# Windowed attention and top-1 experts on one core: the output product as a three-term split with its low part from VectorE, global rows turned ahead of the second pair's queries, and the values of a pair one window at a time

## What is computed

```python
q, k, v = (x @ w.T + b for w, b in ...)          # (2, 2048, 16 heads, 16)
scores = zeros(S, S) per head
scores[window n, window n] = q k^T * scale       # 16 windows of 128 per sequence
scores[gi, gi] += q[gi] k[gi]^T * scale          # gi = 0, 32, 64, ...
out = softmax(scores) @ v @ wo.T + bo
x = layernorm(x + out)
top1 = argmax(x @ Wg.T)
h = gelu((norm(x) * ln_scale[e] + ln_bias[e]) @ W1[e] + b1[e])   # e = top1
x = layernorm(x + h @ W2[e] + b2[e])
```

## Time and profile before

| | us |
|---|---|
| time, median of 3 runs (lowest, highest) | 457.8 (457.61, 458.39) |
| the profiled execution | 456.82 |
| its span, from first to last instruction | 455.1 |
| TensorE busy with matmuls | 413.0 |
| VectorE busy | 331.6 |
| ScalarE busy | 220.6 |
| GpSimd busy | 220.8 |

### The profile page before, as it was taken

How to read it: one execution, slowest core, us unless ns; L and a number is a source line. 1 busy time by engine, 2 the same in 40 slices (tenths; PEclk the granted TensorE clock), 3 DMA queues, 4 the chain that set the end, 5 groups by cost and what they waited for, 6 DMA issues and landing times.

```text
span 455.1 us, 14887 instructions
## 1 busy us (share of the span) xinstructions
PE 413.0 (91%) x5894; PEld 350.1 (77%) x5907; DVE 331.6 (73%) x806; ACT 220.6 (48%) x423; POOL 220.8 (49%) x300
## 2 busy tenths in 40 slices
PE   5968898999999999999999999998799998998981
PEld 4838787898898898898898888776587777877871
DVE  7792578666666666666768888654578899799876
ACT  3413355445446446446446546566664555544320
POOL 5331244535545545545545666436743477458531
PEclk9998999999999999999999999999999999999996
DMA  8650734000000000000002000000000011011112
GB/s 242 193 174 7 211 128 131 26 2 23 23 0 23 23 0 23 23 0 23 23 0 73 24 4 2 3 3 1 0 4 1 0 48 46 5 41 48 46 48 93
DMA packets 21705, 20.35 MB, mean 45 GB/s; under 512 B 3117, under 2 KB 21666, under 8 KB 21666
## 3 DMA queue, kind: packets, MB, share of 16 engines
q1 hardware_dynamic: 17428, 15.60, 10.9%
q10 hardware_dynamic: 4238, 4.22, 3.0%
HBM read 15.41 MB, written 4.41 MB: 44 GB/s over the span
## 4 chain that ended last, share of the span: by engine, by line
PE 69%; DVE 20%; issue 6%; POOL 2%; ACT 1%; DVEq 0%; POOLq 0%; ACTq 0%
PE ps L1413 10%; PE ps L1367 10%; PE ps L1680 7%; PE ps L1376 7%; PE ps L1390 6%; PE ps L1511 6%; PE ps L1358 5%; PE ps L1336 5%; PE ps L1396 4%; PE ps L1381 2%; PE ps L1612 2%; POOL attn_t L594 2%; DVE num_t L1159 2%; DVE row_max_t L1136 1%; DVE hm_part L1287 1%
## 5 line engine op out<-in xcount | busy, mean ns | idle before, releaser
L835 ACT ACTIVATE probs<-ps 128x1024 f32<-128x1024 f32 x64 | 62.1, 1023 | 74.1 <-PE ps L1381 74.1
L1136 DVE TENSOR_REDUCE row_max_t<-ps 128x16 f32<-128x2048 f32 x31 | 70.9, 2288 | 12.7 <-PE ps L1367 12.7
L1680 PE MATMUL ps<-w_part,hm_part 128*128 128x256 f32 x384 | 54.9, 292 | 4.2 <-DVE hm_part L1287 3.7
L1367 PE MATMUL ps<-k_part,q_part 32*128 32x128 f32 x1584 | 51.6, 274 | 3.3 <-issue 1.3
L1367 PEld LDWEIGHTS ps<-k_part,q_part 32*128 32x128 f32 x1584 | 46.9, 186 | 9.5 <-issue 7.0
L594 POOL TENSOR_TENSOR attn_t<-num_t,rden_t 128x256 f32<-128x256 f32 x32 | 19.9, 623 | 70.2 <-DVE rden_t L1162 70.2
L1680 PEld LDWEIGHTS ps<-w_part,hm_part 128*128 128x128 f32 x384 | 48.4, 191 | 7.2 <-DVE hm_part L1287 4.5
L1511 PE MATMUL ps<-xh_parts,w_part 128*128 128x512 f32 x192 | 52.6, 409 | 0.0
L685 ACT ACTIVATE pvT_t<-ps 128x512 f32<-128x512 f32 x34 | 20.4, 599 | 56.5 <-PE ps L1390 53.6
L554 POOL TENSOR_TENSOR q_part<-qf,q_part 128x512 fp32r<-128x512 f32 x32 | 41.5, 1300 | 11.6 <-ACT q_part L685 11.6
L582 POOL TENSOR_TENSOR bounds_t<-guard_t,bounds_t 128x16 f32<-128x16 f32 x32 | 7.1, 222 | 76.6 <-DVE guard_t L1148 76.6
(11 more groups left out here) (226 smaller groups left out, 925.9 us busy)
## 6 DMA issues: line engine op xcount, KB each, us to landing
table<-rest_sums SPq DMA_DIRECT2D x4, 1088.0 KB, 6.8
xs<-in_L_attn_x_dram SPq DMA_DIRECT2D x16, 256.0 KB, 2.7
rows<-in_L_attn_x_dram ACTq DMA_DIRECT2D x4, 1024.0 KB, 7.9
out_dram<-yout SPq DMA_DIRECT2D x7, 512.0 KB, 2.8
w<-in_L_ffn_W_dram SPq DMA_DIRECT2D x2, 256.0 KB, 7.5
w<-in_L_ffn_W_dram SPq DMA_DIRECT2D x1, 512.0 KB, 4.7
out_dram<-yout SPq DMA_DIRECT2D x2, 256.0 KB, 2.1
w_raw<-in_L_attn_wq_dram SPq DMA_DIRECT2D x1, 256.0 KB, 2.9
```

The costliest lines, as they stand in the source:

```text
L835: act.activation(probs[:, 2 * h:2 * h + 2, :], ps[:, 2 * h:2 * h + 2, :], ACT.Exp).then_inc(probs_ready, 1)
L1136: dve.tensor_reduce(row_max[:], ps_all, op=ALU.max, axis=AX.X).then_inc(max_ready, 1)
L1367: last = mm(ps[:, u, (2 * c + a) * P:(2 * c + a + 1) * P], q_part[x][quad(u), s, c, a, :], k_part[y][quad(u), s, c, :], start=(i == 0), st ...
L1680: mm(y, hm_part[a][:, 1 - p, f, c * P:(c + 1) * P], w2_part[b][:, f, :], start=(f == 0 and i == 0), stop=False)
```

## The change

- The output product becomes a split product: `wo` gets a high and a low part like the other weights (`weight_high(WO)` on ScalarE, `w_low(WO)` on GpSimd), and `aT` becomes `aT_part`. ScalarE's copy writes the high part, and a new subtraction on VectorE, between guards and queries, writes the low part; `aT_ready` now comes from VectorE.
- On TensorE the 16 transposes of the global rows and `rest_of_windows` stand ahead of the queries of the second pair in step 0. On VectorE the four `lift` instructions and one on `v_rest` move from before step 0 to behind its guards.
- In odd steps `values_of` does one window of the pair at its old place, `second_values` does the other where x was turned, and x is turned ahead of the turned scores.
- In the expert part `hidden_low` of the last chunk of the last group moves from step 8 to the end of step 7, ahead of `finish(3)`, and in step 8 all twelve Newton steps stand ahead of `finish(0)`; they were spread over the four.
- Some tensors change their place: `vec_rows` and `b1_rows` to an early area, and `wT` of wo into `ffn_rows`.

```diff
         x_part = [sb(f"x_part{i}", [P, KC, 2, P], fp32r) for i in range(2)]
-        w_part = [[sb(f"{n}_part{i}", [P, KC, HID], fp32r) for i in range(2)] for n in ("wq", "wk", "wv")]
+        w_part = [[sb(f"{n}_part{i}", [P, KC, HID], fp32r) for i in range(2)] for n in ("wq", "wk", "wv", "wo")]
         rows = sb("rows", [P, NW * HID])
-        woT = sb("woT", [P, KC, HID])
         out_bias = sb("out_bias", [P, HID])
...
         ffn_rows = sb("ffn_rows", [P, 2, FC * GT])
-        wT = [ffn_rows[:, 0, i * KC * HID:(i + 1) * KC * HID].rearrange("p (c n) -> p c n", c=KC) for i in range(3)] + [woT[:]]
+        wT = [ffn_rows[:, 0, i * KC * HID:(i + 1) * KC * HID].rearrange("p (c n) -> p c n", c=KC) for i in range(4)]
 
...
         rden = sb("rden_t", [P, 2, HEADS])
-        aT = sb("aT_t", [P, KC, P])
+        aT_part = [sb(f"aT_part{i}", [P, KC, P], fp32r) for i in range(2)]
         bn6 = sb("bn6", [P, TG, 6])
...
             pool.iota(rank_i[:], pattern=[[-1, EXPERTS]], base=EXPERTS, channel_multiplier=0).then_inc(late_const, 1)
+            w_low(WO)
             attention_steps(pool, step, first=0, split=2 * SLOTS, between=lambda: pool.wait_ge(other_sums_in_table, 16 * (ROUNDS - 1)))
...
             def weight_high(i):
-                act.wait_ge(wqk_ready, i + 1) if i < WV else act.wait_ge(wvo_ready, 1)
+                act.wait_ge(wqk_ready, i + 1) if i < WV else act.wait_ge(wvo_ready, i - WV + 1)
                 copy(w_part[i][0][:], wT[i]).then_inc(w_high_ready, 1)
...
             values_of(0, 0)
+            weight_high(WO)
             act.wait_ge(g_bound, 1)
...
                     act.wait_ge(aT_in_psum, t - 2)
-                    copy(aT[:].rearrange("p c n -> p (c n)"), ps_rao[:, 0:HID]).then_inc(aT_ready, 1)
+                    copy(aT_part[0][:].rearrange("p c n -> p (c n)"), ps_rao[:, 0:HID]).then_inc(aT_high_ready, 1)
                 if not steady and t == 0:
...
             dve.tensor_tensor(out_bias[:], ps_pv[:, 0:HID], out_bias[:], ALU.add).then_inc(out_bias_ready, 1)
-            for j in range(HPU):
-                dve.scalar_tensor_tensor(lift[:, j, :], global_keys[:], lift_row[:, HPU + 1:HPU + 2],
-                                         lift_row[:, j:j + 1].broadcast_to([P, P]), ALU.mult, ALU.subtract)
-            dve.tensor_scalar(v_rest[:].rearrange("r (h e) -> r h e", e=VA)[:, :, DH], pvals[0:2 * NW, 5:6].broadcast_to([2 * NW, HEADS]),
-                              -float(GLOBALS - GPW), float(S - WINDOW), ALU.mult, ALU.add)
 
...
                     dve.tensor_tensor(guard[:, p, :], row_max[:], at_least, ALU.max).then_inc(guard_ready, 1)
+                if not steady and t == 0:
+                    for j in range(HPU):
+                        dve.scalar_tensor_tensor(lift[:, j, :], global_keys[:], lift_row[:, HPU + 1:HPU + 2],
+                                                 lift_row[:, j:j + 1].broadcast_to([P, P]), ALU.mult, ALU.subtract)
+                    dve.tensor_scalar(v_rest[:].rearrange("r (h e) -> r h e", e=VA)[:, :, DH], pvals[0:2 * NW, 5:6].broadcast_to([2 * NW, HEADS]),
+                                      -float(GLOBALS - GPW), float(S - WINDOW), ALU.mult, ALU.add)
                 if older:
...
                 early(1)
+                if old:
+                    dve.wait_ge(aT_high_ready, t - 2)
+                    dve.tensor_tensor(aT_part[1][:].rearrange("p c n -> p (c n)"), ps_rao[:, 0:HID],
+                                      aT_part[0][:].rearrange("p c n -> p (c n)").bitcast(fp32), ALU.subtract).then_inc(aT_ready, 1)
                 if ahead and p == 0:
...
                                              ps[:, 4 + j % 2, 0:HID], ALU.mult, ALU.add).then_inc(ysum_ready, 1)
-                    newtons(3 * j, 3 * j + 2)
+                    if steady or n != NG:
+                        newtons(3 * j, 3 * j + 2)
                     dve.wait_ge(ysum_ready, w + 1)
...
                 for c in range(FC):
-                    if prev and c == 0:
+                    if prev and c == 0 and (steady or n < NG):
                         hidden_low(n - 1, 1 - p, FC - 1)
...
                         hidden_low(n, p, FC - 2)
+                    if not steady and n == NG - 1 and c == FC - 1:
+                        hidden_low(n, p, FC - 1)
+                    if not steady and n == NG and c == 0:
+                        newtons(0, NEWTON_STEPS + 1)
                     if later and c < 2:
...
                         dve.wait_ge(ybn_ready, 4 * n)
-                    newtons(3 * c + 2, 3 * c + 3)
+                    if steady or n != NG:
+                        newtons(3 * c + 2, 3 * c + 3)
                     if not steady and n == 1:
...
                     pe.wait_ge(w_low_ready, 3)
-                for k in range(2):
-                    last = split_product(ps_kv[:, k * HID:(k + 1) * HID], [part[:, :, k, :] for part in x_part], w_part[WV])
-                last.then_inc(v_in_psum, 1)
+                split_product(ps_kv[:, 0:HID], [part[:, :, 0, :] for part in x_part], w_part[WV])
+
+            def second_values():
+                split_product(ps_kv[:, HID:2 * HID], [part[:, :, 1, :] for part in x_part], w_part[WV]).then_inc(v_in_psum, 1)
 
...
                 pe.wait_ge(aT_ready, w + 1)
-                product(ps_rao[:, HID:2 * HID], lambda c: aT[:, c, :], lambda c: woT[:, c, :]).then_inc(o_in_psum, 1)
+                if isinstance(w, int) and w == 0:
+                    pe.wait_ge(w_low_ready, 4)
+                split_product(ps_rao[:, HID:2 * HID], aT_part, w_part[WO]).then_inc(o_in_psum, 1)
 
...
                     sum_windows()
+                if not steady and t == 0:
+                    pe.wait_ge(gs_shifted, B)
+                    pe.wait_ge(max_ready, 1)
+                    for u in range(UNITS):
+                        for i in range(HPU):
+                            last = nc.tensor.transpose(ps[:, u, i * P:(i + 1) * P], dg[:, u, i * P:(i + 1) * P], ident[:])
+                    last.then_inc(gT_in_psum, 1)
+                    rest_of_windows()
                 if not steady and t == 1:
...
                     values_of(t + 1)
+                if live(t + 3, steady) and p:
+                    turn_x(t + 3)
                 if not steady and t == NW - 2:
...
                     last.then_inc(b1_sums_in_psum, 1)
-                if not steady and t == 0:
-                    pe.wait_ge(gs_shifted, B)
-                    pe.wait_ge(max_ready, 1)
-                    for u in range(UNITS):
-                        for i in range(HPU):
-                            last = nc.tensor.transpose(ps[:, u, i * P:(i + 1) * P], dg[:, u, i * P:(i + 1) * P], ident[:])
-                    last.then_inc(gT_in_psum, 1)
-                    rest_of_windows()
                 if not steady and t == 1:
...
                     keys_of(t + AHEAD)
-                if live(t + 3, steady) and p:
-                    turn_x(t + 3)
+                if live(t + 1, steady) and p:
+                    second_values()
                 if pp:
...
             values_of(0)
+            second_values()
             pe.wait_ge(gs_scaled, B)
...
             pe.wait_ge(consts_ready, 1)
-            product(ps_pv[:, 0:HID], lambda c: bv_wide[:, c, :], lambda c: woT[:, c, :]).then_inc(bias_in_psum, 1)
+            product(ps_pv[:, 0:HID], lambda c: bv_wide[:, c, :], lambda c: wT[WO][:, c, :]).then_inc(bias_in_psum, 1)
             attention_steps(pe, step, first=0)
```

More of the change, by code:

```diff
@@ L117, in windowed_attention_then_top1_experts @@
             colvals = early_sb("colvals", [P, 2, 2 * NW])
+            vec_rows = early_sb("vec_rows", [NVEC, HID])
+            b1_rows = early_sb("b1_rows", [FC, P])
         w1_part = [sb(f"w1_part{i}", [P, KC, EXPERTS * EH], fp32r) for i in range(2)]
@@ L192, in windowed_attention_then_top1_experts @@
         nx = sb("newton_x", [P, NW])
-        vec_rows = sb("vec_rows", [NVEC, HID])
         vecT = sb("vecT", [P, KC, NVEC])
         bq_col, bk_col, bv_col = (vecT[:, :, 3 * EXPERTS + i] for i in range(3))
-        b1_rows = sb("b1_rows", [FC, P])
         w1 = sb("w1", [P, KC, EXPERTS, EH])
@@ L361, in windowed_attention_then_top1_experts @@
         aT_in_psum = sem("aT_in_psum")
+        aT_high_ready = sem("aT_high_ready")
         aT_ready = sem("aT_ready")
```

## The result

The changed kernel takes 459.8 us (median of 7 runs, 458.6 to 460.7) against 458.3 us for the kernel before, run beside it (median of 7, 457.5 to 459.0). The ratio is 1.0037, with a 95% interval from 1.0021 to 1.0053: 0.4% slower. The forecast was 450.0 us, with a range from 445.0 to 455.7, so both its size and its sign are wrong.

What follows compares the result with a forecast made beforehand. TensorE was taken to pace the attention loop, with long single waits at start and end. Start -5.5, loop -5.6 and end +3.3 made -7.8 us: 449.0 for the profiled execution, 450.0 for the median, range 445.0 to 455.7.

Steps and rivals of the forecast that it cites:

- Start, -5.5: Up to the scores of window 2: global rows turned earlier, at full clock, gain 5.5 us, bounds 3.4 and 6.5.
- into idle time of both: Start: the split of wo, a ScalarE copy and a GpSimd subtraction, falls into idle time of both engines.
- Loop, even steps, 0: Attention loop: VectorE's added instruction changes nothing in even steps; bad end 0.15 us each, 2 us in all.
- third rival: Even steps: VectorE paces the loop, its added 0.42 us delaying every step, +11.8 us, 467 us in all; chance 0.06.
- Loop, odd steps, -0.4 each: Attention loop: moved values and x shorten 14 odd steps from 8.20 to 7.81 us, 5.6 us in all.
- The old stall is gone: Odd steps: 1.73 us of TensorE work behind the sums covers the 1.75 us until the attention transposes can start.
- End, +3.3: Expert end: Newton chain ahead of window 28's sum idles TensorE 5.3 us; loss 3.3 us, bounds -3 and 4.5.
- Nothing I can price changes: Between loop and end: no change priced; output products there stand behind waits for routing and residuals.
- first rival: Loop gives nothing: row maxima in odd steps and numerators in even ones take back 0.4 us; 455.6 us, chance 0.16.

Runs made afterwards that it cites:

- e4: Changed kernel with the output product in fp32 again (no split, no parts of wo), all else kept: 454.6 us.
- e11: Kernel before with only the global rows turned ahead of the second pair's queries and the lift instructions behind the first guards: 451.9 us.
- e7: Changed kernel with VectorE's new low part, in even steps, ahead of the row maxima instead of ahead of the queries: 458.6 us.
- e8: Changed kernel with the two attention transposes of an odd step behind the scores of the next even step: 455.8 us.
- e1: Changed kernel with both edits of the end undone (last hidden chunk's low part and Newton steps at their old places): 456.7 us.
- e3: Changed kernel with the twelve Newton steps of group 6 behind the sum of window 29, not ahead of that of window 28: 455.1 us.
- e2: Changed kernel with only the Newton steps back in their old places, the last hidden chunk's low part still early: 456.9 us.
- e6: Changed kernel with both windows' values together at the old place and x turned where it was before: 459.2 us.
- e5: Changed kernel with only GpSimd's subtraction for wo moved behind its low part of the first pair's queries in step 0: 457.5 us.
- e9: Changed kernel without the output product's split and with the Newton steps of group 6 behind the sum of window 29: 449.8 us.
- e10: Changed kernel without the split, group 6 Newton steps behind window 29's sum, odd steps' attention transposes behind the next scores: 446.7 us.
- e12: Kernel before with only the output product split (low part on VectorE, parts of wo at the start): 462.2 us.

## Why the prediction was wrong, step by step

- **Start, -5.5: right where the split isn't.** e4 and e11 show its terms (31.34, full clock, window 2 at 46.8 and 47.1). The step that failed is the half-sentence that put the split of wo "into idle time of both" engines. It priced the instruction where it stands, not what it does to its neighbour: 1.32 us on `g_row`, and in this profile 1.63 of clock behind it. From `g_row` on, the change gains 2.42 us, and e4 5.41. The earlier trace rows held the pattern (a 0.17 us instruction at 1.82 beside GpSimd), and the forecast used it at the end but not at the start.
- **Loop, even steps, 0: wrong by 3.2 us.** The step that failed is the wait of the bounds' turning on the numerators: I put it at 0 to 0.15 us and let 0.06 us saved cancel it. Measured, the ordinary even step is +0.15, and in every other one, where VectorE's bounds come 0.17 us later than in the rest (4.33 us after the scores, not 4.16), +0.26 to +0.38: before, a small slack had hidden that difference, and the numerators started 6.18 to 6.20 us after the scores in both. It is the third rival's place at a quarter of its price, but not its wait: the keys did cover the attention transposes of even steps, as I had said against it. e7 shows it by taking the instruction out of the chain, e8 by bringing TensorE there later.
- **Loop, odd steps, -0.4 each: 0.1.** "The old stall is gone" was nearly true (by e8, 0.05 us of it is left in the loop), but I counted it as time gained. The timelines give, from start of the sums to the transposes, 2.43 us before and 2.42 after: the drain, numerators, reciprocal and division take that long whatever TensorE does meanwhile, so the moved values fill that time and don't shorten it. My step had 0.60 + 0.81 + 0.11 + 0.81 = 2.33 there, 0.22 for the transposes (0.34), and 3.95 ahead of the turned scores (4.03). Three terms were small by 0.08 to 0.12, and together they are the missing 0.3; for the transposes itself has 0.41. The whole gain is in front, where 4.13 became 4.03 at the row maxima. That new wait I had forecast at 0.20 us; it is 0.27 (4.03, less 3.76 of scores, weighing, values and x).
- **End, +3.3: right in mechanism and size.** 5.10 us idle (5.3), sum of window 28 at 444.78 (444.9), half clock behind it, +2.83 in all; e1 gives 3.1 in the medians.
- **Left out:** the 1.5 us between loop and experts. "Nothing I can price changes" was true of the instructions; the six matmuls behind the routing ran at the lower clock level.
- **The chances.** 0.06 for VectorE pacing the even steps was too little: the text itself said that these had no hole, and the first rival's two places (row maxima in odd steps, numerators in even ones) are where the gain went. Rival one's 0 for the loop was the better centre, with losses on its far side.

## What to carry to other kernels

An instruction added to an engine costs nothing only where that engine has a hole between its input and the next thing somebody waits for; in a step whose instructions follow without one, count its full length until a slack is shown to absorb it. Filling a wait with moved work gains only what leaves the place it came from. Measure a stall from start to start across the whole chain of other engines that ends it, not from the end of a piece of the chain of waits, and ask whether the moved work touches that chain at all. Small VectorE tensor_scalars that overlap with a long GpSimd instruction must be priced with it: `g_row` and the Newton steps shown here ended only when it ended, while VectorE's residual, with one input in PSUM, kept its 0.42 us beside the division. And a block of small dependent steps belongs behind the reads that free TensorE's banks.

## What was not expected of the hardware

The clock after an idle time of 2.3 to 2.8 us went either way. The 16 turned global rows at the start took 3.60, 3.50 and 3.58 us after idle times of 2.75, 2.27 and 2.76 us (after, e1, e8), 2.79 and 2.94 after 2.74 and 2.75 (e3, e7), but 1.97 after 2.48 and 2.75 (e2, e6); after 1.19 to 1.43 us it was 1.96 or 1.97 each time (e4, e5, e9, e10, e11). The six matmuls behind the routing took 1.65 or 1.66 us in four profiles (before, e6, e11, e12) and 1.94 to 2.93 in the ten others, after idle times of 2.48 to 2.65 us in both sets. e6, after 2.65 us:

```profile
329.48 0.39 PE L1481 MATMUL ps<-ident_b,onehot 128*24 128x128 bf16 x4 [2.65 <-DVE onehot L1108]
329.80 1.65 PE L1526 MATMUL ps<-xh_parts,w_part 128*128 128x512 f32 x6
```

The four are the profiles without the values edit, yet the instructions ahead of the wait are the same in e6 and in the changed kernel, and e6's ten executions ranged in mean granted clock from 0.975 (462.9 us) to 0.993 (458.5 us). Whether the edit has a part in it, or chance alone, stays open. In e8 the clock fell at a third place, after an idle time of 0.84 us, and two of its ten executions, at a mean clock of 0.990, took 451.8 and 452.4 us where the other eight took 454.9 to 456.5. What the rows do show is the price: 1.2 to 1.7 us each time the clock falls at one of these places.
